# Decoder layer on one core: the first half's rows sorted into blocks of one expert each, instead of all experts over all rows

## The reference, cut to what matters

```python
x = x + attn(layernorm(x))                      # self, causal, 16 heads
x = x + xattn(layernorm(x), ctx_768)            # 6404 keys
x = x + ffn(layernorm(x))
# ffn:
logits = einsum('bsd,de->bse', x, router_w) + router_b
topk_scores, topk_idx = top_k(logits, 2)
topk_gates = softmax(topk_scores)               # two gates per row
combine = einsum('bsk,bske->bse', topk_gates, one_hot(topk_idx, 8))
for e in range(8):                              # every expert over every row
    h = relu(x @ W1[e] + b1[e])                 # 128 -> 512
    out += (h @ W2[e] + b2[e]) * combine[..., e:e+1]
```

## Time and profile before

| what | us |
|---|---|
| median of 3 runs | 1004.61 |
| the profiled execution's time | 1005.74 |
| its span | 1003.8 |
| PE busy | 875.2 (87%) |
| ACT busy | 868.0 (86%) |
| DVE busy | 167.5 (17%) |
| POOL busy | 9.1 (1%) |

### The profile page before, as it was taken

How to read it: one execution, slowest core, us unless ns; L and a number is a source line. 1 busy time by engine, 2 the same in 40 slices (tenths; PEclk the granted TensorE clock), 3 DMA queues, 4 the chain that set the end, 5 groups by cost and what they waited for, 6 DMA issues and landing times.

```text
span 1003.8 us, 14820 instructions
## 1 busy us (share of the span) xinstructions
PE 875.2 (87%) x6128; PEld 257.4 (26%) x6128; DVE 167.5 (17%) x432; ACT 868.0 (86%) x664; POOL 9.1 (1%) x33
## 2 busy tenths in 40 slices
PE   6977889998888888888899888888888888899997
PEld 4552322221111111111122211111111111134443
DVE  5764543420000000000013000000000000033212
ACT  4666978999999999999999999999999999933342
POOL 3000000000000000000000000000000000000000
PEclk9987999999999999999999999999998999999999
DMA  4251007211211111111221111112221000020200
GB/s 142 106 184 43 2 17 215 69 32 42 45 41 39 35 35 33 32 39 43 45 41 36 32 32 36 35 34 46 40 44 35 1 1 2 1 86 1 84 10 11
DMA packets 19716, 46.31 MB, mean 46 GB/s; under 512 B 6210, under 2 KB 9388, under 8 KB 19132
## 3 DMA queue, kind: packets, MB, share of 16 engines
q1 hardware_dynamic: 19644, 45.31, 17.7%
HBM read 38.18 MB, written 7.11 MB: 45 GB/s over the span
## 4 chain that ended last, share of the span: by engine, by line
PE 35%; ACT 31%; issue 31%; DVE 2%; DMA 1%; SPq 0%; ACTq 0%; DVEq 0%
ACT probs L710 31%; PE psum L1370 10%; PE psum L1334 6%; PE psum L1590 6%; PE psum L1602 5%; PE psum L1226 1%; PE psum L1266 1%; PE psum L1270 1%; PE psum L1486 1%; DVE turned L929 1%; PE psum L1366 1%; PE psum L1253 1%; PE psum L1472 0%; DMA ctx_region<-in_ctx 0%; PE psum L1210 0%
## 5 line engine op out<-in xcount | busy, mean ns | idle before, releaser
L710 ACT ACTIVATE probs<-psum 128x1536 f32<-128x1536 f32 (+1 forms) x520 | 784.1, 1777 | 30.0 <-PE psum L1334 15.9
L1370 PE MATMUL psum<-probs,v_ctx 128*9 128x512 f32 x3200 | 422.7, 600 | 3.1 <-DVE turned L929 2.7
L1334 PE MATMUL psum<-q_all,k_ring 32*128 32x512 f32 (+1 forms) x1792 | 265.1, 493 | 105.5 <-ACT probs L710 102.5
L1334 PEld LDWEIGHTS psum<-q_all,k_ring 32*128 32x128 f32 x1792 | 102.7, 185 | 501.2 <-ACT probs L710 453.6
L929 DVE STREAM_TRANSPOSE turned<-psum 128x512 f32<-128x512 f32 x16 | 11.5, 717 | 625.9 <-PE psum L1366 609.0
L762 ACT ACTIVATE probs<-psum,b_sb 128x512 f32<-128x512 f32 x64 | 44.0, 687 | 71.8 <-PE psum L1590 71.7
L1370 PEld LDWEIGHTS psum<-probs,v_ctx 128*9 128x9 f32 x3200 | 47.6, 88 | 104.7 <-issue 97.5
L1590 PE MATMUL psum<-xnT,w_region 128*128 128x512 f32 x128 | 65.3, 594 | 1.7 <-issue 1.7
L1602 PE MATMUL psum<-probs,ctx_region 128*128 128x512 f32 x128 | 65.0, 592 | 0.0
L1370 PE MATMUL psum<-probs,v_self 128*9 128x512 f32 (+3 forms) x384 | 41.1, 528 | 2.0 <-DVE probs L950 1.4
L1602 PEld LDWEIGHTS psum<-probs,ctx_region 128*128 128x128 f32 x128 | 24.3, 190 | 30.6 <-issue 30.6
(11 more groups left out here) (144 smaller groups left out, 248.1 us busy)
## 6 DMA issues: line engine op xcount, KB each, us to landing
k_ring<-kc_parts SPq DMA_DIRECT2D x256, 52.0 KB
k_ring<-kc_parts SPq DMA_DIRECT2D x256, 48.0 KB
kc_parts<-kparts_bc SPq DMA_DIRECT2D x8, 512.0 KB, 2.8
probs<-gate_rows SPq DMA_DIRECT2D x4, 1024.0 KB, 5.9
kc_parts<-probs SPq DMA_DIRECT2D x4, 512.0 KB, 2.8
w_region<-in_L_ffn_W SPq DMA_DIRECT2D x1, 2048.0 KB, 9.3
ctx_region<-in_ctx SPq DMA_DIRECT2D x1, 768.0 KB, 8.9
ctx_region<-in_ctx SPq DMA_DIRECT2D x1, 672.0 KB, 7.5
```

The source lines that it names most:

```text
L710: act.activation(probs[:, slot:slot + w, :], psum[:, at:at + w, :], ACT.Exp, scale=SC[ph]).then_inc(L[ph]["exp_done"], 1)
L1334: mm = pe.matmul(into[:, col:col + n_q], keys, q_all[rows, g, hf * HALF + q0:hf * HALF + q0 + n_q], start=True, stop=True)
L1370: mm = pe.matmul(into[:, q0:q0 + w], v_all[:, h, t, :], probs[:, place(ph, at)[1], col:col + w], start=first, stop=last)
```

## The change

For the first half only, the dense sweep over 8 experts is replaced by sorted blocks. 512 rows with 2 experts each are 1024 (row, expert) pairs; each expert's pairs are padded to a multiple of 128, which gives at most 15 blocks of 128 rows with one expert each.

PE counts rows per expert (`count_rows`), DVE works out the slot of each pair and the expert of each block (`places_of_rows`), POOL scatters the rows to DRAM with 8 indirect transfers, loads the 15 blocks back, and copies each block's W1 and W2 slices inside SBUF (`to_experts`). PE transposes the blocks and works on 11 of them beside the second half's attention, one hidden and one output piece per block, 8 groups apart; the relu and the copies of these are on DVE. The last 4 blocks run after the attention, with the relu on ACT. Then the second half runs through all 8 experts as before, with four output banks instead of two. POOL stores the outputs, gathers two rows per row back with 8 indirect transfers, and DVE combines them with the gates (`first_half_together`). The groups from 274 on are 3 and 3 banks wide (231 groups) instead of 4 and 3 (198 groups), which frees the side bank.

```diff
-                                (len(PLANS[1][0]) - FIRST_BANKS - BESIDE_AGAIN, (4, 3))), NEXT_SLOT)
+                                (len(PLANS[1][0]) - FIRST_BANKS - BESIDE_AGAIN, (3, 3))), NEXT_SLOT)
+BLOCKS = 2 * HALF // P + E - 1
+EARLY = 11
+B2_AT, COUNT_AT, TURN_AT, HIDDEN_AT = (SUMMED_AT + n for n in (33, 37, 60, 78))
+BLOCK_STEP, OUTPUT_STEP = 16, 8
...
+            sp.wait_ge(s["consts_made"], N_CONSTS)
+            sp.dma_start(xs_dram.rearrange("(j p) d -> p j d", p=P), zeros[:, :].unsqueeze(1).to_broadcast([P, BLOCKS, D]))\
...
+            def to_experts(fast):
+                pool.wait_ge(s["xs_cleared"], 16)
+                pool.wait_ge(s["block_done"], block_step("counts"))
+                for n in range(2 * 4):
+                    pool.indirect_dma_start(xs_dram[:, :], bass.IndirectOffsetOnAxis(slots[:, n:n + 1], 0),
+                                            xn[:, n % 4, :], None).then_inc(s["rows_moved"], 16)
+                pool.wait_ge(s["rows_moved"], ROWS_PLACED)
+                pool.dma_start(blocks[:, 0:BLOCKS, :], xs_dram.rearrange("(j p) d -> p j d", p=P))\
+                    .then_inc(s["rows_moved"], 16)
...
+                for j in range(BLOCKS):
+                    w1_at, w2_at, loaded, _ = weights_of(j)
+                    if 2 <= j < EARLY + 2:
+                        pool.wait_ge(s["block_ps"], block_step("output", j - 2))
...
+                    e = pool.value_load(expert_at[0:1, j:j + 1], min_val=0, max_val=E - 1)
+                    pool.dma_start(w1_at, w1_region[:, bass.ds(e * FF, FF)]).then_inc(loaded, 16)
+                    pool.dma_start(w2_at, ctx_region[:, bass.ds(e * NF * D, NF * D)]).then_inc(loaded, 16)
...
+                pool.wait_ge(s["block_done"], block_step("output", BLOCKS - 1))
+                store(EARLY, BLOCKS - EARLY)
+                pool.wait_ge(s["rows_moved"], OUTPUTS_STORED)
+                for n in range(2 * 4):
+                    pool.indirect_dma_start(got[n // 4][:, n % 4 * D:(n % 4 + 1) * D], None, ys_dram[:, :],
+                                            bass.IndirectOffsetOnAxis(slots[:, n:n + 1], 0)).then_inc(s["rows_moved"], 16)
...
+            late_relu(EARLY)
+            for j in range(EARLY + 1, BLOCKS):
+                late_relu(j)
+                late_output(j - 1)
+            late_output(BLOCKS - 1)
-            for n in range(NHALF * E * NF):
+            for n in range(E * NF):
...
+            def turn_block_rows(q):
+                pe.wait_ge(s["rows_moved"], ROWS_LOADED)
...
+            def hidden_of_block(j, into):
+                w1_at, _, loaded, value = weights_of(j)
+                pe.wait_ge(loaded, value)
+                for f in range(NF):
+                    mm = pe.matmul(into[:, f * P:(f + 1) * P], w1_at[:, f * P:(f + 1) * P], blocks[:, j, :],
+                                   start=True, stop=True)
+            def output_of_block(j, into):
+                _, w2_at, _, _ = weights_of(j)
+                for f in range(NF):
+                    mm = pe.matmul(into, block_hidden[j % 2][:, f * P:(f + 1) * P], w2_at[:, f * D:(f + 1) * D],
+                                   start=(f == 0), stop=(f == NF - 1))
...
+            for q in range(-(-BLOCKS // 4)):
+                first_routed[TURN_AT + 4 * q] = lambda q=q: turn_block_rows(q)
+            for j in range(EARLY):
+                first_routed[HIDDEN_AT + BLOCK_STEP * j] = lambda j=j: early_hidden(j)
+                first_routed[HIDDEN_AT + BLOCK_STEP * j + OUTPUT_STEP] = lambda j=j: early_output(j)
...
+            late_hidden(EARLY)
+            for j in range(EARLY + 1, BLOCKS):
+                late_hidden(j)
+                late_output(j - 1)
+                if j == EARLY + 1:
+                    project_heads(2, 1, wox_sb, CHAIN_BANK)
+            late_output(BLOCKS - 1)
+            transpose_norm(1, 6, CHAIN_BANK)
+            pe.wait_ge(s["normT_done"], 4 + NHALF)
...
-            for n in range(NHALF * E * NF + LAG):
-                if n < NHALF * E * NF:
+            for n in range(E * NF + LAG):
+                if n < E * NF:
                     hidden_units(n)
```

More of the change, by code:

```diff
@@ L44 @@
 NF = FF // P
+BLOCKS = 2 * HALF // P + E - 1
+EARLY = 11
+LATE_BANKS = (2, 4, 5, 6)
 SELF_SCALE = float(D) ** -0.5
@@ L596, in _ @@
             after(pool.memset(ktail_quads[:, :].bitcast(F32), 0.0), "consts_made")
+            after(pool.memset(ones[:, :], 1.0), "consts_made")
+            after(pool.memset(zeros[:, :], 0.0), "consts_made")
+            after(pool.memset(both[:, 4, :], 0.0), "consts_made")
+            after(pool.memset(below[:, :, :], 1.0))
+            after(pool.affine_select(out=below[:, :, :], in_=below[:, :, :], compare_op=ALU.is_ge, fill=0.0, base=-1,
+                                     pattern=[[1, E], [-1, E]], channel_multiplier=0), "consts_made")
+            for j in range(BLOCKS + 1):
+                after(pool.memset(block_no[:, j:j + 1], float(j)), "consts_made")
             for e in range(E):
@@ L958, in normalise @@
                 while n < len(ends):
+                    if ph == 1 and n >= QUADS:
+                        for group in sorted(block_work):
+                            if ends[n - 1][3] <= group < ends[n][3]:
+                                block_work[group]()
                     unit(n)
@@ new lines, in block_output @@
+            def block_output(j):
+                dve.wait_ge(s["block_ps"], block_step("output", j))
+                dve.tensor_copy(blocks[:, j, :], bank(SIDE_BANK)[:, 0:D]).then_inc(s["block_done"], 1)
+            block_work = {TURN_AT + 4 * q: (lambda q=q: block_rows_turned(q)) for q in range(-(-BLOCKS // 4))}
+            for j in range(EARLY):
+                block_work[HIDDEN_AT + BLOCK_STEP * j] = lambda j=j: block_relu(j)
+                block_work[HIDDEN_AT + BLOCK_STEP * j + OUTPUT_STEP] = lambda j=j: block_output(j)
@@ new lines, in _ @@
+            second_half_rows()
+            rows_turned(1, 4, CHAIN_BANK)
+            router_rows(1, CHAIN_BANK)
+            two_experts(1, CHAIN_BANK)
+            two_gates(1)
+            gates_turned(1, CHAIN_BANK)
+            for e in range(E):
+                dve.wait_ge(s[f"gate_rows{e // (E // 2)}"], 16)
+                dve.wait_ge(s["hid_used"], (e + 1) * NF)
+                dst = yT[:, 1, :] if e == 0 else rest[:, :]
+                step(dve.scalar_tensor_tensor(dst, bank(4 + e % 4), b2T_sb[:, e:e + 1], gate_rows[:, e, :],
@@ new lines, in count_rows @@
+            def count_rows():
+                pe.wait_ge(s["picked"], 1)
+                pe.wait_ge(s["block_done"], block_step("biases"))
+                pe.matmul(bank(SIDE_BANK)[:, 0:5 * E], causal[:, :], both[:, :, :].rearrange("p b e -> p (b e)"),
+                          start=True, stop=False)
+                for b in range(4):
+                    mm = pe.matmul(bank(SIDE_BANK)[:, (b + 1) * E:5 * E], ones[:, :],
+                                   both[:, b:b + 1, :].to_broadcast([P, 4 - b, E]), start=False, stop=(b == 3))
+                mm.then_inc(s["block_ps"], 1)
```

260 lines of the change are left out of this document (198 added, 62 removed).

## The result

The changed kernel takes 975.63 us (median of 4 runs, 973.38 to 977.88) against 1003.54 us (4 runs, 1001.83 to 1005.69): 0.971 of the time before, interval 0.9678 to 0.9742. Forecast were 976.5 us, with 966 to 992 as the range. The profiled execution took 975.13 us, its span 973.4.

The account below looks back on a forecast made before the run. ACT's exponentials were taken to pace the attention and PE the stage behind it. Attention +17.0 and the stage behind -45.1 gave -28.1 us: span 1003.8 to 975.7, median 976.5 us, range 966 to 992.

Parts of the forecast that it names:

- The end stage: Behind the attention: 32 slices removed (55.0 us), first dense matmul 11.9 us later; the stage 45.1 us shorter.
- the three things: Behind the attention: waits that could arise, such as for gate rows and gathers, were costed at nothing.
- The attention: Work added beside the second half's attention: +3.1 + 13.2 + 0.7 = +17.0 us.
- term (b): Beside the attention: 22 block pieces behind sums, 0.6 us each, +13.2 us (6.6 to 24).
- term (a): From group 274: 3-wide groups, 231 exponentials at 1.34 us, with unit ends and clock dips, +3.1 us.
- term (c): Beside the attention: four pieces of transposes, the bias and the count pieces, about 0.1 us each, +0.7 us.
- The stall (d): PE's first transposes, group 297, waiting for POOL's scatters and load: 0 us taken, within a 28.6 us window.
- R1: Rows come late at group 297: 5 to 28 us more, time 982 to 1004; chance 0.13.
- R2: Pieces beside the attention cost their full 1.09 us or more, PE being nearly full: 987 us; chance 0.08.
- R3: Pieces beside the attention are nearly free, 0.2 to 0.3 us each: 970 us; chance 0.07.
- R4: Slower than before: scatters one after the other at over 6.6 us each stall group 297; 1018 at 8 us; chance 0.05.
- R5: Late blocks fail to cover DVE's chain, or gates and gathers come late: +5 to +10 us, 984; chance 0.05.

Follow-up runs that it names:

- e1: The kernel before with only the groups from 274 on made 3 and 3 banks wide instead of 4 and 3: 1005.38 us, ratio 1.0015.
- e5: The changed kernel run again unchanged, to see whether the pause belongs to it: 977.44 us, ratio 0.9748.
- e12: The changed kernel with the count 8 groups later and the first transposes 8 groups earlier: 989.27 us, ratio 0.984.
- e8: The changed kernel with pieces and transposes in groups without sums, and after the attention the projection and its transposes earlier: 962.7 us, ratio 0.9605.
- e9: e8 with the second four scatters waiting on POOL for the first four to land: 958.6 us, ratio 0.9536.
- e6: The changed kernel with the count, and so the scatters, 8 groups later, transposes unmoved: 982.61 us, ratio 0.9782.
- e10: e8 with each scatter waiting for the one before to land, transposes and pieces 8 groups later: 958.68 us, ratio 0.9542.
- e11: e8 with the eight scatters replaced by plain 64 KB transfers to fixed rows, leaving the rows unsorted: 958.55 us, ratio 0.9551.
- e2: The changed kernel with the block pieces one group earlier, in the group without sums: 966.32 us, ratio 0.962.
- e4: The changed kernel with the transposes of the blocks 8 groups earlier: 979.71 us, ratio 0.9749.
- e3: The changed kernel with each block piece cut in two, four groups apart, both still behind sums: 971.02 us, ratio 0.9661.
- e7: The changed kernel with the block pieces two groups later, ahead of the group without sums: 978.63 us, ratio 0.9751.

## Why the prediction was right, step by step

**The end stage** was worked out as 78.5 us behind the last exponential and is 78.5. The slices, the chain on DVE (xn done at 908.6, 13.8 us after the last exponential; forecast 894.0 - 880.2 = 13.8), the first dense matmul (15.3 us against 15.5) and the three things costed at nothing (gates, gathers, blocks' weights) hold. -45.1 is right.

**The attention** from group 274 to the last exponential took 894.88 - 567.08 = 327.8 us. Forecast were 311.4 + 17.0 = 328.4, but the 0.7 us of idle that goes stands ahead of group 274 (568.84 in the earlier trace rows comes to 568.1), so the terms inside the stretch add up to 329.1. They were less good than their sum.

- The pieces, term (b), were the step with the wrong size: 22 x 0.75 = 16.5 instead of 13.2. The 0.6 was read where a piece stands every third group; the price is the lateness of the next scores, 1.09 us, less the reserve of 0.34.
- The width, term (a): 307.6 (230 x 1.331 + 1.5) and 3.1 of unit ends are 310.7; against 311.4, and with the 0.7 ahead of it, that is -1.4 instead of +3.1. I had rounded the distance up to 1.34 (2.1 us over 230 groups) and allowed 5.5 us for unit ends and dips of the clock, but this profile had none of the dips there. e1 bounds the width at -1 to +4 us.
- The small pieces, term (c): 0.73 in gaps, forecast 0.7.

So +15.8 instead of +17.0: two misses of 3.3 and 4.5 us had opposite signs, and that the total came so close is partly luck. Another 0.9 us is the spread between two executions: the first exponential of the cross-attention starts at 67.82 here, at 69.31 in e5's profile of the same kernel and at 68.73 in the kernel before. Together, -45.1 + 15.8 - 0.9 is within 0.2 us of the -30.4 between the two spans; the forecast of 975.7 was 2.3 above the 973.4.

**The stall (d)** is 0 as forecast, but my reading of it was thin. The first scatter is at 573.58 (forecast 573.2), the blocks are there 20.6 us later, PE comes at 601.15 (forecast 601.8). The Trainium skill (DMA: Bandwidth & Descriptors, "Anatomy of one DMA — SWDGE (gpsimd) path") led to an estimate of 21.5 us, close in sum; its parts were not: the eight scatters take 11.55 us until POOL goes on (573.58 to 585.13), overlapped, not 17, and the load 9.1, not 4.3 (in e12 6.3, and the whole 17.9). e12 shows what would have come without the window.

**What the prediction did not have** is the pause. It is none of the rivals: R1 put the loss at PE's transposes, and it sits ahead of them, on ACT (at groups 284 to 286, where the scatters are not moved). In the first profile it is absent; in the others it is 1.6 us and more. e8 to e9 price it at 4.1 us of the median in that version, and at 4.9 us between the two profiles. Why the changed kernel's own two sets of runs (975.63 and 977.44) show little of it, and its neighbours in time more, stays open, and so does what holds ACT: the trace names no engine, and the instruction loads of the period look the same with and without the pause. That POOL's row of scatters makes it is shown by e6 (it moves with them) and by e9 and e10 (it goes when the row is broken up). Whether it takes the indirect form, as e11 suggests, or only a long unbroken row, is not shown.

**The rivals.** R2 was nearest in kind (the lateness is the full 1.09) but not in price. R3's price was reached only where the pieces stand in PE's wait (e2, e8 and those behind it). R1, R4 and R5 did not occur: a scatter costs 1.27 us, not 6.6.

## What to carry to other kernels

A piece of foreign work beside a loop that another engine paces costs the lateness of the very next thing that engine needs, less its reserve. Put it into the slot in which the host engine waits anyway: here a shift by one group took 22 pieces from 16.5 us to some 2, and a shift by two groups the other way gained nothing. Check a predicted wait by its own row and not by the total: in e4 the total agreed while the wait was not there. And a row of merged instructions without gaps is not free of loss: divide its length by its count, as in e3.

## What the runs showed of the hardware

- An indirect transfer of 64 KB from POOL takes 0.96 us to issue, one every 1.27 us; a plain one of the same size 0.56 us. The last of eight has landed 2.5 us after its start (POOL goes on at 585.13, from 582.61).
- In eight of nine profiles with eight indirect ones in a row, ACT stops for 1.4 to 2.9 us (twice in e6), which costs up to 5.9 us with what follows; in the one profile with a wait for landing behind the fourth this is gone (962.7 to 958.6 us in the medians).
- PE's idle time of 2.77 us went with 6.8 us at the lower clock, which began 0.65 us before PE started again; PE was busy in the rest of them. With an idle time of 1.40 us the clock fell in e7 and did not in e5.
- A load of 960 KB in rows of 512 bytes from POOL's queue lands after 9.1 us in the first profile and after 6.3 us in e12's; the 1024 KB of the earlier trace rows took 5.9.
